# A four-layer network on one core: eight table entries, one early pass of score biases and one value unit are put elsewhere

## The reference, cut to what matters

```
layer 0 attention:  q, k, v = x@Wq, x@Wk, x@Wv          (16 heads of 64)
                    out = softmax(q k' / 8 + slope_h (i - j), causal) @ v @ Wo + bo
layer 0 ffn:        x @ weight' + pooled(x) @ disha
layer 1 attention:  states_k = (x + x@Wk_k)' (x + x@Wv_k) / N,  state = states_0 * states_1
                    out = layernorm((x + x@Wq) @ state) @ Wo + bo
layer 1 ffn:        gates = softmax(x @ wg'), the best 8 of 64 experts for each row,
                    rank of each row inside its expert, at most 160 rows an expert,
                    sum of the experts' swiglu rows + a shared swiglu
```

## Time and profile before

| | |
|---|---|
| median of three runs | 2101.25 us |
| profiled execution, its own time | 2099.48 us |
| its span | 2097.4 us |
| TensorE busy | 2058.9 us, 98% |
| VectorE, ScalarE, GpSimd busy | 45%, 39%, 40% |
| chain that ended last | 92% on TensorE |
| granted TensorE clock | full in all 40 slices |

### The profile page before, as it was taken

How to read it: one execution, slowest core, us unless ns; L and a number is a source line. 1 busy time by engine, 2 the same in 40 slices (tenths; PEclk the granted TensorE clock), 3 DMA queues, 4 the chain that set the end, 5 groups by cost and what they waited for, 6 DMA issues and landing times.

```text
span 2097.4 us, 37509 instructions
## 1 busy us (share of the span) xinstructions
PE 2058.9 (98%) x11780; PEld 1539.2 (73%) x11780; DVE 946.0 (45%) x3719; ACT 823.7 (39%) x2122; POOL 840.8 (40%) x958
## 2 busy tenths in 40 slices
PE   9999999999999999999999999999999999999998
PEld 5555666566656656666667666899999999999956
DVE  3536556565574574566546523222222222222236
ACT  5746646645556475466564112111111111111110
POOL 3436527437356276275274604122222223222332
PEclk9999999999999999999999999999999999999999
DMA  6800002100100000000003201477888788778841
GB/s 206 254 1 11 11 22 77 45 15 22 36 20 13 32 16 4 33 20 19 12 17 129 98 11 44 158 259 264 269 267 265 263 270 266 260 263 260 279 113 60
DMA packets 101731, 245.69 MB, mean 117 GB/s; under 512 B 22412, under 2 KB 78187, under 8 KB 93240
## 3 DMA queue, kind: packets, MB, share of 16 engines
q1 hardware_dynamic: 75448, 224.09, 29.6%
q0 software_dynamic: 26112, 19.55, 5.8%
HBM read 193.97 MB, written 87.91 MB: 134 GB/s over the span
## 4 chain that ended last, share of the span: by engine, by line
PE 92%; DVE 3%; ACT 3%; issue 2%; POOL 0%; DVEq 0%; ACTq 0%; POOLq 0%
PE bank L1934 20%; PE bank L1543 10%; PE bank L1947 10%; PE bank L1589 8%; PE bank L1579 7%; PE bank L1554 7%; PE bank L1841 6%; PE bank L1565 5%; PE bank L1534 5%; PE bank L1853 4%; ACT pT L788 2%; PE bank L1626 1%; PE bank L1634 1%; PE bank L1602 1%; PE bank L1642 1%
## 5 line engine op out<-in xcount | busy, mean ns | idle before, releaser
L681 POOL TENSOR_TENSOR prob<-prob,rsum 128x512 f32<-128x512 f32 (+3 forms) x512 | 350.1, 715 | 486.5 <-DVE rsum L1091 486.3
L1934 PE MATMUL bank<-pT,big_w 128*128 128x160 f32 x3072 | 438.2, 299 | 0.0
L1934 PEld LDWEIGHTS bank<-pT,big_w 128*128 128x128 f32 x3072 | 422.7, 190 | 0.1
L804 ACT ACTIVATE prob<-prob,negmax 128x512 f32<-128x512 f32 (+3 forms) x512 | 284.5, 564 | 216.8 <-DVE negmax L1082 216.8
L687 POOL DMA_INDIRECT disp<-send,slot x288 | 283.1, 983 | 189.9 <-DVE slot L1268 102.6
L733 POOL DMA_INDIRECT acc<-qk,token_e x64 | 99.1, 1548 | 488.2 <-ACT qk L964 185.3
L1082 DVE CUSTOM_DVE_ANT_0 prob<-bank,bias 128x512 f32<-128x512 f32 (+3 forms) x512 | 220.8, 487 | 155.6 <-PE bank L1554 145.1
L957 ACT ACTIVATE pT<-bank 128x480 f32<-128x480 f32 x128 | 73.0, 570 | 458.8 <-PE bank L1934 458.8
L1543 PE MATMUL bank<-xT,big_w 128*128 128x512 f32 x512 | 245.3, 602 | 2.6 <-ACT v_s L788 1.7
L1406 DVE TENSOR_TENSOR pT<-pT,bank 128x480 f32<-128x480 f32 x128 | 83.8, 654 | 335.9 <-PE bank L1934 335.8
L1947 PE MATMUL bank<-pT,big_w 128*128 128x160 f32 x1536 | 219.3, 300 | 0.0
(11 more groups left out here) (195 smaller groups left out, 2378.9 us busy)
## 6 DMA issues: line engine op xcount, KB each, us to landing
big_w<-ew SPq DMA_DIRECT2D x64, 1536.0 KB, 7.0
big_w<-ew SPq DMA_DIRECT2D x64, 768.0 KB, 5.5
disp<-send SPq DMA_DIRECT2D x1, 10272.0 KB, 39.6
xT<-disp SPq DMA_DIRECT2D x64, 160.5 KB, 5.3
disp<-send,slot POOLq DMA_INDIRECT x288
x<-x SPq DMA_DIRECT2D x8, 512.0 KB, 3.9
x_d<-x SPq DMA_DIRECT2D x8, 512.0 KB, 2.7
hT_d<-hT SPq DMA_DIRECT2D x8, 512.0 KB, 2.6
```

The lines of the kernel that those rows point to most:

```text
L681: i = g.tensor_tensor(pr, pr, rsum[:, n, j:T].rearrange("p (t a) -> p t a", a=1).to_broadcast([P, T - j, P]), ALU.mult)
L804: a.activation(prob_rows(n, t), prob_rows(n, t), ACT.Exp, bias=negmax[:, n, t:t + 1], scale=-1.0, accum_out=psumm[:, n, t:t + 1]).then_inc ...
L1934: i = mm(bank[2 * half + 1 - part][:, q * CAP:(q + 1) * CAP], w1[:, c, f * P:(f + 1) * P], xbT[:, c], start=(c == 0), stop=(c == C - 1), s ...
```

## The change: what it does

Four things are edited.

1. `L2` of pair 0 of the following batch is issued in step 0, slot B, ahead of the `slots` operations (and in the first batch in the same slot with nothing behind it). Step 1 leaves it out in all batches but the first.
2. In `batch_end` the value unit that used to be hung at slot `k` of step 0 (V3) moves to slot `e`, and there it stands between the ranks and the wait for `ranks_read`.
3. Other parts are hung elsewhere. TensorE and the ring: V4 from (1, q) to (1, b), V5 from (2, b) to (1, k), V6 from (4, b) to (3, k), V7 from (4, k) to (4, e), L0 from (4, e) to (5, k), `state` from (5, q) to (5, k), `fuse` from (5, k) to (6, b), `l1o_T` from (6, e) to (7, b). ScalarE: its copy for `moe_T` from (0, q) to (0, k). VectorE: the rsqrt of the next x from the end of step 4 to slot A of step 5, its scaling from (5, A) to (5, C). The remaining edits of `VECTOR_AT` name a later or earlier slot of the same step with nothing in between.
4. ScalarE's list: `T00` before `E00`, `T12` before `E10`, and `E12` behind `O` and the slot `e`.

```diff
-        TENSOR_AT = {... (5, 'q'): ('state',), (5, 'k'): ('fuse',), ... (6, 'e'): ('l1o_T',), ...
+        TENSOR_AT = {... (5, 'k'): ('state',), (6, 'b'): ('fuse',), ... (7, 'b'): ('l1o_T',), ...
-        RING_AT = {(1, 'q'): (('V', 4),), (2, 'b'): (('V', 5),), (4, 'b'): (('V', 6),), (4, 'k'): (('V', 7),), ...
+        RING_AT = {(1, 'b'): (('V', 4),), (1, 'k'): (('V', 5),), (3, 'k'): (('V', 6),), (4, 'e'): (('V', 7),), ...
-        SCALAR_STEP = ('F03', 'F13', 'P0', 'b', 'q', 'E00', 'T00', 'E01', 'P1', 'T01', 'T02', 'T10', 'T11', 'k', 'E02',
-                       'E10', 'T12', 'E11', 'E12', 'O', 'e')
+        SCALAR_STEP = ('F03', 'F13', 'P0', 'b', 'q', 'T00', 'E00', 'E01', 'P1', 'T01', 'T02', 'T10', 'T11', 'k', 'E02',
+                       'T12', 'E10', 'E11', 'O', 'e', 'E12')
...
             def extras(g, at_slot, p, following):
+                if g == 0 and p is None and at_slot == "B":
+                    bias_round(following, 0, 2)
                 if p is not None:
                     for part in VECTOR_AT.get((g, at_slot), ()):
+                        if part == "slots":
+                            bias_round(following, 0, 2)
                         post(p, part)
...
                     elif part[0] == "L":
-                        bias_round(*prev, 2)
+                        if g != 1 or a[0] is None and a[1] == 0:
+                            bias_round(*prev, 2)
...
                     leave(range(T // 2))
-                    for key in units[:1]:
-                        ring_unit(a, key, p, following)
                     post(p, "rank")
-                    for key in units[1:]:
+                    for key in units:
                         ring_unit(a, key, p, following)
```

More of the change, by code:

```diff
@@ L285, in bass_sandwich @@
         TENSOR_AT = {(2, 'e'): ('ffn_T',), (3, 'q'): ('ffn',), (4, 'e'): ('gram',), (5, 'b'): ('t1',), (5,
-                   'q'): ('state',), (5, 'k'): ('fuse',), (6, 'q'): ('rows',), (6, 'e'): ('l1o_T',), (7,
+                   'k'): ('state',), (6, 'b'): ('fuse',), (6, 'q'): ('rows',), (7, 'b'): ('l1o_T',), (7,
                    'q'): ('l1wo',), (0, 'q'): ('moe_T',), (0, 'e'): ('logits',)}
         SCALAR_AT = {(2, 'e'): ('ffn_T',), (4, 'e'): ('gram',), (5, 'q'): ('t1',), (6, 'b'): ('fuse',), (6,
-                   'e'): ('l1o_T',), (0, 'q'): ('moe_T',), (0, 'e'): ('gates',)}
-        VECTOR_AT = {(1, 'B'): ('wo_norm', 'x1_sum'), (2, 'A'): ('x1_norm',), (3, 'B'): ('ffn_sum', 'ffn_norm',
-                   'x2_sum'), (4, 'B'): ('x2_norm',), (5, 'B'): ('state',), (6, 'B'): ('l1_sum',), (6,
-                   'C'): ('l1_norm',), (7, 'A'): ('l1o_sum', 'l1o_norm', 'x3_sum'), (7, 'B'): ('x3_norm',), (0,
+                   'e'): ('l1o_T',), (0, 'k'): ('moe_T',), (0, 'e'): ('gates',)}
+        VECTOR_AT = {(1, 'B'): ('wo_norm', 'x1_sum'), (2, 'A'): ('x1_norm',), (3, 'B'): ('ffn_sum', 'ffn_norm'), (3,
+                   'C'): ('x2_sum',), (4, 'C'): ('x2_norm',), (5, 'B'): ('state',), (6, 'A'): ('l1_sum',), (6,
+                   'C'): ('l1_norm',), (7, 'A'): ('l1o_sum', 'l1o_norm', 'x3_sum'), (7, 'C'): ('x3_norm',), (0,
                    'B'): ('gates1', 'gates2', 'slots')}
-        X_AT = {(2, 'A'): 'means', (4, 'B'): 'rsqrt', (5, 'A'): 'scale'}
-        RING_AT = {(1, 'q'): (('V', 4),), (2, 'b'): (('V', 5),), (4, 'b'): (('V', 6),), (4, 'k'): (('V', 7),), (4,
-                   'e'): (('L', 0),), (6, 'b'): (('L', 1),), (6, 'k'): (('X', 0), ('X', 1)), (7, 'k'): (('V', 0), ('V',
-                   1)), (0, 'b'): (('V', 2),), (0, 'k'): (('V', 3),)}
+        X_AT = {(2, 'B'): 'means', (5, 'A'): 'rsqrt', (5, 'C'): 'scale'}
+        RING_AT = {(1, 'b'): (('V', 4),), (1, 'k'): (('V', 5),), (3, 'k'): (('V', 6),), (4, 'e'): (('V', 7),), (5,
+                   'k'): (('L', 0),), (6, 'b'): (('L', 1),), (6, 'k'): (('X', 0), ('X', 1)), (7, 'k'): (('V', 0), ('V',
+                   1)), (0, 'b'): (('V', 2),), (0, 'e'): (('V', 3),)}
         EARLY_RING = (("X", 0), ("X", 1), ("P", 0, 0), ("P", 0, 1), ("V", 0), ("V", 1), ("P", 1, 0), ("V", 2),
```

## The result

The changed kernel takes 2085.77 us (median of four runs, 2085.17 to 2086.47), the kernel before 2100.32 us beside it (four runs, 2099.26 to 2101.30). The ratio is 0.993 with a 95% interval of 0.9918 to 0.9942: 14.6 us faster. The forecast was 2088.0 us. The profiled execution took 2085.34 us, its span is 2083.3 us, the clock is granted in full.

The account below looks back on a forecast made before the run. TensorE, busy 98% of the span, was taken as the bound, so only its waits could be won: three terms of 18.3 us less 2.7, 1.0 and 1.3 give 13.3, hence 2088.0 us; eight in ten from 2082.5 to 2096.0.

Parts of the forecast that it names:

- likeliest case: Whole kernel: the forecast of 2088.0 us holds, with a range of 2085 to 2091 us; chance 0.57.
- Term 1: Step 1's second score stage: issuing L2 of pair 0 early removes its wait for negmax, 1.58 us a turn, 10.7 us.
- S1 still waits: Rival, step 1's second score stage: something else in VectorE's or ScalarE's queue holds it; 2096 us, chance 0.07.
- Term 2: k projection in step 1: V4 one unit earlier removes the wait for ScalarE's copy, 0.36 us seven times, 2.5 us.
- Term 3: Turn between batches: V3 fills the output projection's wait of 0.84 us for ranks_read, six times, 5.1 us.
- The price in step 2: Step 2's transposes: products lead T00 by only 1.4 us, costing 0.4 us in each of seven batches, 2.7 us.
- the dear bound: Step 2: if the VectorE and GpSimd overlap costs as much as before, lead 0.85 us, price 0.95, together 6.6 us.
- The price in step 4: Step 4: V7 no longer stands before T12, so 0.3 us paid becomes about 0.45, 7 x 0.15 = 1.0 us.
- Step 4 keeps its chain: Step 4: the lead hangs on ffn_sum, with V6 between the ffn and T00 before and after the change.
- Little things: Other moved parts and ScalarE's order, together with the last batch: 1.3 us in all, bounds 0 and 4.
- E00: Last batch: this exponential stands in front of T01's copy with no P1 to cover it, costing 0.5 us once.
- ScalarE's new order makes it slower: Rival, steps 2 and 4: later O and F exponentials shrink the lead by 2.2 us; 2109 us, chance 0.06.

Follow-up runs that it names:

- V5's experiment: The changed kernel with value unit V5 moved back from (1, k) to (2, b): 2194.86 us on a later chip, ratio 0.9902 to the kernel before there.
- B: One of the three later chips; the changed kernel, run again unaltered there, took 2191.29 us, ratio 0.9886 to the kernel before.

## Why the prediction was right, by its steps

The sign, the mechanism and the size held: the forecast is 2.2 us above the measured median, which lies inside the range of the likeliest case (2085 to 2091), near its lower end. Part of the closeness is luck: two terms were mis-sized and cancel, the ranks by 0.27 us in six places (1.6 us too little gain) and step 4 by 0.22 in seven (1.5 us too little price). By steps:

- *Term 1* (1.58 us a turn) is there: S0 with S1 went from 3.51 to 1.92 us, and the pass alone gives 1.45. What failed is the reason as far as it was told of the change as a whole: "S1 starts ... because L2 of pair 0 runs at 295.72" names one of two cures, and V4 ahead of the scores is the other. The case *S1 still waits* was weaker than its chance of 0.07: even without the pass S1 does not wait.
- *Term 2* (0.36): T00 to P1 went from 0.85 to 0.50 us.
- *Term 3* (0.84) was mis-sized. From the first record of the ranks to P0 it was 8.42 us (283.88 to 292.30) and is 9.11 (281.44 to 290.55), of which 1.80 are V3's own (281.84 to 283.64): 7.31, so 1.11 gained, 0.27 more than the named gap. Term 1 had exactly this 0.27 added to its named gap, and term 3 should have had it too. With 1.59, 0.35 and 1.11 the three terms are 3.05 of the 3.19 us by which S0 to S2 shortened in this turn. The rest was in no term: V3 no longer covers the copy in front of T12 in step 0 (0.18 us lost from S0 to the ranks), and V4, V5 and P1 in their new places give 0.32. The value unit alone gives 0.84 in its trace, where an issue gap of 0.18 us stands in front of P0 that the full change doesn't have.
- *The price in step 2* (0.4, bounds near 0 and 0.95) measured 0.38. Its working held as well: products at 309.05 were forecast in the times of the kernel before, and 307.28 + 1.75 = 309.03 came; T00 was put at 310.5 and came at 310.30, so the lead was 1.27 us in this turn instead of 1.4 (1.41 in the middle of five). Both parts of the 1.0 us are there: R0 starts 0.51 us earlier than before by the same clock (297.66 to 295.40 + 1.75; 0.4 was taken), and of the 128x4 operations beside the products there are three (0.72, 0.32 and 0.54 us) instead of four (0.65, 0.74, 0.32 and 0.55), each 0.16 afterwards, which is 0.52 less (0.6 was taken). That a lead "under about 1.7 us is paid nearly in full", with 0.1 for the last product, is borne out by the 1.79 of the ledger. The sum at the dear bound has a slip: it is 13.3 - 3.9 = 9.4 us, not 14.3 - 3.9.
- *The price in step 4* (0.15, bounds 0 and 0.5) was mis-sized too: 0.37 us from S4 to S6. "Step 4 keeps its chain" is the step that did not hold: the lead went from 1.44 to 1.23 us. From the ffn's first record (the two rows below, before and after) to T00 it is 16.16 and 16.05 us, the gain of V6's new place, and to the products 14.72 and 14.82: both take from the lead. By the 1.79 of the ledger a lead shorter by 0.24 (1.46 to 1.22 in the middle of five turns) is 0.24 of the 0.37; the other 0.13 would be V7, which no longer covers the copy in front of T12 (an estimate). ScalarE does not set the products here: F waits 0.56 us for VectorE.

```profile
324.35 3.72 PE L1589 MATMUL bank<-weff,xTp 128*128 128x256 f32 x16
...
320.84 3.72 PE L1594 MATMUL bank<-weff,xTp 128*128 128x256 f32 x16
```

- *Little things* (1.3 us in all): V5 and V6, said to "bring no work", do bring something. In front of T12 each saves 0.12 us, by the cover of the copy behind the last transposes. E00 in the last batch (0.5 us once) is there: TensorE waits 0.96 us for a copy of the transposes at 1107.63 us, before 0.33 at 1121.86.
- The turn was put at 143.6 to 143.9 us and is 143.16, outside that sign. Of the 14.1 us between the two profiled executions five turns give 11.9, the first batch 1.75, the rest of the kernel about half a microsecond.
- *ScalarE's new order makes it slower*: the order costs 0.4 us in step 4 on the later chips, far from the 2.5 us there that this case needed, and is paid for in step 0. V5's experiment shows that its main premise was wrong: whether a value unit stands behind O or in front of it moves the lead by 0.1 to 0.4 us, not by its 1.8.

## What to carry to other kernels

Where a wait stands at the turn of a loop, look for every instruction ahead of the late one in its own engine's queue, and for work that can stand ahead of the waiting one; either may be enough, and only a trial of each alone tells what the other adds. A pass moved forward in an in-order queue pushes everything it passes: find what else behind that block is awaited (here the reciprocals) before moving it, and place it behind the last instruction that has to wait anyhow. Compare product to product on the slower engine with step to step on TensorE: the difference is what the lead loses in each step.

## What the runs showed of the hardware that I had not expected

The three later chips take 116 to 129 us more for the kernel before, and B takes 106 more for the changed kernel. Its trace there is 108 us longer: 8 before the first S0 of the loop, 48 in the five turns, 52 behind them. TensorE has stops which the trace on the chip of the forecast does not have at these places. In the loop they stand in steps 3 to 6; with the waits that both traces have they come to 38 us in the five turns, against 5.5 there:

```profile
PE bank L1530 <- issue: 13.5, 6, 3.3
PE bank L1570 <- ACT xT L788: 10.7, 6, 2.2
...
PE bank L1594 <- ACT xTp L788: 8.5, 6, 1.7
```

They come at the same lines in every turn. Others follow behind the loop, in the shared network (two lines with 15.9 and 10.7 us). In the loop they go with stops of ScalarE that no engine of the profile ends ("remote"): in step 3, 2.24 us before the copy that L1594 waits for, and 3.03 us before the copy ahead of it:

```profile
326.48 0.60 ACT L788 ACTIVATE oT<-bank 128x512 f32<-128x512 f32 x1 [3.03 <-remote]
329.32 1.09 ACT L788 ACTIVATE xTp<-bank 128x512 f32<-128x512 f32 x2 [2.24 <-remote]
```

In the second of two such stops the clock falls. TensorE in step 6 of the same trace:

```profile
392.68 0.66 PE L1530 MATMUL bank<-ident,xa 128*128 128x128 f32 x4 [1.92 <-issue]
395.56 0.69 PE L1570 MATMUL bank<-ident,prob 128*128 128x128 f32 x2 [2.22 <-ACT xT L788]
396.18 1.22 PE L1559 MATMUL bank<-qk 64*128 64x256 f32 x4
397.33 4.21 PE L1584 MATMUL bank<-pT,v_s 128*64 128x512 f32 x16
```

The windows of this stretch (columns as in the earlier trace rows) have the granted clock at 1.00 up to 394 us, 0.63 from 394 to 395, 0.50 from 395 to 401, the lower of the two levels (1.2 GHz), and 0.98 and 1.00 behind it:

```profile
395.00:396.00 1.00, 0.44 (x2) 0.29 (x2) 0.00 (x0) 1.00 (x3) 0.00 (x0) 0.50 0.00 0
396.00:398.00 2.00, 2.00 (x8) 0.80 (x8) 0.40 (x3) 1.96 (x7) 0.00 (x0) 0.50 0.03 8
...
401.00:403.00 2.00, 2.00 (x10) 0.84 (x7) 0.00 (x0) 0.60 (x1) 0.00 (x0) 0.98 0.00 0
```

The sixteen matmuls of O last 4.21 us there and 2.37 at full clock. So 4.1 us of waiting cost another 1.8 us in this row alone. It falls so in other turns of this trace too (0.57 from 547 to 553, 0.54 from 853 to 859, 0.52 from 1005 to 1011). Of the 48 us that the five turns are longer, the added waits are 33, and TensorE's busy time is 725.7 us in place of 710.1 for the same 3751 records, which is likely the lower clock. What the stops are, and why three chips have them and the chip of the forecast had not, stays open; no experiment was made on it.
